# Second feed-forward of a routed macaron block: dispatched rows carry the residual, finished rows are scattered into the output, and one accumulating DMA closes it

## The reference, cut to what matters

```
def ffn(x, up, gate, down, router, w_up_s, w_gate_s, w_down_s):   # 8 experts, hidden 256
    idx = argmax(x @ router.T)                 # one expert for each row
    y  = (silu(x @ gate[idx].T) * (x @ up[idx].T)) @ down[idx].T
    ys = (silu(x @ w_gate_s.T) * (x @ w_up_s.T)) @ w_down_s.T      # shared expert, all rows
    return y + ys

x = x + 0.5 * ffn(layernorm(x), ...)
x = x + attn(layernorm(x), ...)                # attn(z) = z + gate * circular mixing of a decayed sum over t
x = x + 0.5 * ffn(layernorm(x), ...)
```

## Time and profile before

| | |
|---|---|
| the three times | 354.20, 349.97, 352.72 us; median 352.72 |
| span of the profiled execution | 305.8 us |
| median less that span | 46.9 us |
| mean granted clock of TensorE | 0.952 |
| PE, DVE, ACT, POOL busy in the span | 254.6, 187.3, 161.7, 194.1 us |
| DMA | 28.34 MB |

### The profile page before, as it was taken

The page is one execution under the profiler, slowest core; times in us unless marked ns, Lnnn a source line. Parts: engine busy times, 40 slices in busy tenths (PEclk is TensorE's granted clock), DMA queues, the critical chain, the costliest instruction groups (busy, mean ns, idle before and its releaser), DMA issues.

```text
span 305.8 us, 7883 instructions
## 1 busy us (share of the span) xinstructions
PE 254.6 (83%) x1788; PEld 213.2 (70%) x1788; DVE 187.3 (61%) x723; ACT 161.7 (53%) x376; POOL 194.1 (63%) x307
## 2 busy tenths in 40 slices
PE   0588999945999999994589888989779999999950
PEld 0446777535999999963468666757479989999540
DVE  4267574951565656537799999776646655565334
ACT  2455544232676777622769777940357766675100
POOL 3358887760478788861365888877408868788500
PEclk9999999995999999998957999999999999999976
DMA  7861111322223332218100111112322323332198
GB/s 201 287 287 35 46 43 46 102 71 62 58 86 97 88 97 87 78 46 248 28 3 1 35 38 35 47 45 70 101 64 80 90 72 96 87 96 64 48 289 253
DMA packets 34990, 28.34 MB, mean 93 GB/s; under 512 B 4784, under 2 KB 31792, under 8 KB 34704
## 3 DMA queue, kind: packets, MB, share of 16 engines
q1 hardware_dynamic: 25328, 16.06, 18.7%
q0 software_dynamic: 4544, 9.45, 8.6%
q10 hardware_dynamic: 5088, 2.50, 2.8%
HBM read 15.37 MB, written 12.62 MB: 92 GB/s over the span
## 4 chain that ended last, share of the span: by engine, by line
PE 42%; POOL 24%; DVE 10%; issue 9%; DMA 7%; ACT 3%; SPq 2%; DVEq 1%; POOLq 0%; ACTq 0%
PE bank L949 22%; POOL dispatched L374 15%; PE bank L959 9%; POOL scale_f L363 4%; PE bank L883 3%; PE bank L938 3%; POOL returned L404 2%; DMA back<-returned 2%; DVE xres L599 2%; DMA decay<-in_decay 2%; PE bank L895 1%; DMA returned<-ey,token 1%; PE bank L875 1%; DMA xs<-dispatched 1%; DVE hs L631 1%
## 5 line engine op out<-in xcount | busy, mean ns | idle before, releaser
L404 POOL DMA_INDIRECT returned<-ey,token x78 | 78.1, 1002 | 33.6 <-DVE ey L799 21.8
L949 PE MATMUL bank<-xsT,wgu 128*128 128x128 f32 x624 | 84.4, 280 | 2.8 <-ACT xsT L524 1.7
L949 PEld LDWEIGHTS bank<-xsT,wgu 128*128 128x128 f32 x624 | 77.0, 195 | 4.3 <-ACT xsT L524 1.5
L374 POOL DMA_INDIRECT dispatched<-xn,slot x64 | 63.9, 998 | 18.0 <-issue 18.0
L875 PE MATMUL bank<-xnT,gu 128*128 128x512 f32 x128 | 63.2, 620 | 4.6 <-DVE hs L631 3.7
L793 DVE TENSOR_TENSOR eh<-eg,bank 128x256 f32<-128x256 f32 x78 | 32.8, 421 | 49.3 <-ACT eg L531 36.5
L531 ACT ACTIVATE eg<-bank 128x256 f32<-128x256 f32 x78 | 29.9, 383 | 37.9 <-PE bank L949 37.7
L505 ACT ACTIVATE wgu<-gu 128x512 f32 x78 | 48.3, 624 | 0.9 <-issue 0.8
L959 PE MATMUL bank<-wdn,eh 128*128 128x128 f32 x312 | 47.4, 276 | 0.7 <-DVE ey L799 0.7
L480 ACT ACTIVATE sg<-bank 128x512 f32<-128x512 f32 x32 | 18.7, 589 | 49.2 <-PE bank L875 41.7
L883 PEld LDWEIGHTS bank<-dn,hs 128*128 128x128 f32 x256 | 33.4, 209 | 12.2 <-DVE hs L631 10.8
(11 more groups left out here) (100 smaller groups left out, 287.1 us busy)
## 6 DMA issues: line engine op xcount, KB each, us to landing
xs<-dispatched SPq DMA_DIRECT2D x80, 66.0 KB, 1.8
back<-returned SPq DMA_DIRECT2D x16, 256.0 KB, 5.4
gu<-in_gu SPq DMA_DIRECT2D x1, 2048.0 KB, 12.1
out<-xres ACTq DMA_DIRECT2D x8, 256.0 KB, 3.5
returned<-ey,token POOLq DMA_INDIRECT x78, 2.3
dn<-in_dn SPq DMA_DIRECT2D x1, 1024.0 KB, 10.9
dispatched<-xn,slot POOLq DMA_INDIRECT x64, 2.3
dispatched<-pads SPq DMA_DIRECT2D x10, 66.0 KB
```

The costliest lines, as they stand in the source:

```text
L374: nc.gpsimd.indirect_dma_start(dispatched[:, :], bass.IndirectOffsetOnAxis(slot[:, i:i + 1], 0), xn[:, i, :], None, bounds_check=last_row) ...
L404: nc.gpsimd.indirect_dma_start(returned[:, :], bass.IndirectOffsetOnAxis(token[:, s:s + 1], 0), ey[:, s, :], None, bounds_check=last_back) ...
L949: last = nc.tensor.matmul(bank[4 + s % WR][:, i * P:(i + 1) * P], wgu[:, s % WR, i * P:(i + 1) * P], xsT[:, s // 2 % 2, s % 2, :], start=T ...
```

## The change

- `xn` and `xres` become two parts of one buffer `rows`, 260 wide. There are two DRAM tensors, `dispatched[0]` with rows of 132 and `dispatched[1]` with rows of 260 that carry normed row, number and residual.
- In the second feed-forward the residual that is sent must hold the shared expert's result. So `parts_at(1, ...)` gives each step three parts, 19 in the steps, and the last 5 stand before the experts; none stands behind. POOL sends group k in step k+2 for k below 6, waiting for `half_done`; group 6 in step 7 ahead of group 5; group 7 last. Groups 6 and 7 are sent with a residual that has no shared part yet: their shared results go to `shared_late`.
- In both feed-forwards there are no tokens: the scatter of block b takes its index straight from `xs`. Pad rows all have the number N and are dropped by the bounds check. A block beyond the real ones loads 128 dummy rows. `load_block` waits `blk_out[s]` (the scatter of the slot's earlier block has landed) where it waited `blk_tok`.
- In the second, DVE evicts 0.5 y + residual, and the scatter goes to the output itself. Loads of `back`, adds and stores go. POOL waits for all scatters, and adds `shared_late` to groups 6 and 7 of the output with one accumulating DMA.

```diff
+WIDE = ROW + C
+DUMMY = E * CAP
+LATER_STEP = 3
+BASED = G - 2
+BEFORE = 3 * BASED + 1
...
+        rows = sb("rows", [P, NT, WIDE])
+        xn, xres = rows[:, :, 0:ROW], rows[:, :, ROW:WIDE]
+        shared_late = sb("shared_late", [P, (G - BASED) * TPG, C])
...
-        def parts_at(k, i):
-
-            return SHARED_PARTS[PER_STEP * (k - 1) + i:][:1] if 1 <= k < G else []
+        def parts_at(f, k, i):
+
+            if not 1 <= k < G:
+                return []
+            if f == 0:
+                return SHARED_PARTS[PER_STEP * (k - 1) + i:][:1]
+            first = LATER_STEP * (k - 1)
+            cut = (first, first + 1, first + LATER_STEP)
+            return SHARED_PARTS[cut[i]:min(cut[i + 1], BEFORE)]
+
+        def parts_before(f):
+
+            return (SHARED_PARTS[EARLY:LATE] if f == 0 else SHARED_PARTS[BEFORE:])
...
@@ load_block (SP)
                 wait_pos(sp, blk_turn, f * (NBL // 2) + (j - 1) * PAIRS + s // 2 + 1)
                 stand(sp)
-                first_use = is_int(j) and j == 0
-                wait_pos(sp, blk_tok, f * NB if first_use else f * NB + b - BU + 1)
+                wait_pos(sp, blk_out[s], (f * slot_blocks(s) + j) * 16)
                 stand(sp)
                 if row is None:
                     row = block_row(b)
-                sp.dma_start(xs[:, s, :], dispatched[bass.ds(row, P), :]).then_inc(blk_in[s], 16)
+                sp.dma_start(xs[:, s, 0:row_width(f)], dispatched[f][bass.ds(row, P), :]).then_inc(blk_in[s], 16)
...
                 sp.wait_ge(pads_at, f + 1)
-                send_pads(sp, range(0, PADS_SP))
+                sp.dma_start(dispatched[f][DUMMY:DUMMY + P, :], pads[:, 0:row_width(f)]).then_inc(pad_sent, 16)
+                send_pads(sp, f, range(0, PADS_SP))
...
-                for k in range(G):
-                    sp.dma_start(tiles(back, k),
-                                 returned_tiles[:, k * TPG:(k + 1) * TPG, :]).then_inc(back_in[k], 16)
-            sp.wait_ge(stored, 16 * G)
+                if f == 0:
+                    for k in range(G):
+                        sp.dma_start(tiles(back, k),
+                                     returned_tiles[:, k * TPG:(k + 1) * TPG, :]).then_inc(back_in[k], 16)
+            sp.wait_ge(stored, 16)
...
@@ POOL: scatter, middle, experts
                 pool.wait_ge(slotted, f * G + k + 1)
+                if f == 1 and k < BASED:
+                    pool.wait_ge(half_done, G + k + 1)
...
-                if valid(k):
-                    scatter(1, k)
+                if k == G - 1:
+                    scatter(1, BASED)
+                if 0 <= k - 2 < BASED:
+                    scatter(1, k - 2)
...
-                def tokens(j, s):
-
-                    pool.wait_ge(blk_in[s], (f * LOADS + j + 1) * 16)
-                    wait_pos(pool, blk_out[s], (f * slot_blocks(s) + j) * 16)
-                    nc.gpsimd.tensor_tensor(token[:, s:s + 1], xs[:, s, C:C + 1].bitcast(I32),
-                                            to_replica[:, bass.ds(j * BU + s, 1)], ALU.add).then_inc(blk_tok, 1)
-
-                def send(j, s):
-                    pool.wait_ge(blk_tok, f * NB + j * BU + s + 1)
+                target = out_rows if f else returned[:, :]
+
+                def send(j, s, more=True):
                     pool.wait_ge(blk_y, f * NB + j * BU + s + 1)
                     stand(pool)
                     nc.gpsimd.indirect_dma_start(
-                        returned[:, :], bass.IndirectOffsetOnAxis(token[:, s:s + 1], 0),
-                        ey[:, s, :], None, bounds_check=last_back).then_inc(blk_out[s], 16)
+                        target, bass.IndirectOffsetOnAxis(xs[:, s, C:C + 1].bitcast(I32), 0),
+                        ey[:, s, :], None, bounds_check=last_token, oob_is_err=False).then_inc(blk_out[s], 16)
...
             steps(middle, 4)
+            for k in range(BASED + 1, G):
+                scatter(1, k)
             experts(1)
+            for s in range(BU):
+                pool.wait_ge(blk_out[s], 16 * slot_blocks(s) * 2)
+            pool.wait_ge(half_done, 2 * G)
+            nc.gpsimd.dma_start(out_dram[:, BASED * TPG:NT, :], shared_late[:], accum_op=ALU.add).then_inc(stored, 16)
...
@@ ACT, end
-            for g, part in SHARED_PARTS[LATE:]:
-                shared(1, g, part)
-            for k in range(G):
-                act.wait_ge(x3_done, k + 1)
-                act.dma_start(out_dram[:, k * TPG:(k + 1) * TPG, :], tiles(xres, k)).then_inc(stored, 16)
...
@@ DVE: add_shared, tables, evac_y
-                add_half(k, by_tile(o_ps[:]), half_done)
+                if n >= G and k >= BASED:
+                    nc.vector.tensor_scalar(tiles(shared_late, k - BASED), by_tile(o_ps[:]), 0.5, None,
+                                            ALU.mult).then_inc(half_done, 1)
+                else:
+                    add_half(k, by_tile(o_ps[:]), half_done)
...
-                link(nc.vector.tensor_scalar(last_blk[:], blk_end[:, E - 1:E], -1.0, None, ALU.add))
-
-                link(nc.vector.tensor_scalar(real_blk[:], block_no[:], last_blk[:], None, ALU.min))
...
-                    nc.vector.tensor_copy(ey[:, s, :], bank[2 + s % 2][:, 0:C]).then_inc(blk_y, 1)
+                    y = bank[2 + s % 2][:, 0:C]
+                    if f == 0:
+                        nc.vector.tensor_copy(ey[:, s, :], y).then_inc(blk_y, 1)
+                    else:
+
+                        nc.vector.scalar_tensor_tensor(out=ey[:, s, :], in0=y, scalar=0.5, in1=xs[:, s, ROW:WIDE],
+                                                       op0=ALU.mult, op1=ALU.add).then_inc(blk_y, 1)
...
@@ DVE, end
-            for g, part in SHARED_PARTS[LATE:-2]:
-                shared(1, g, part)
-            for k in range(G):
-                add_back(1, k, x3_done)
-                if k < 2:
-                    shared(1, *SHARED_PARTS[k - 2])
...
@@ PE, experts
-                pe.wait_ge(half_done, f * G + parts_done(LATE, down=True))
-                pe.wait_ge(mult_done, f * G * HH + parts_done(LATE, down=False))
+                done = len(SHARED_PARTS) if f else LATE
+                pe.wait_ge(half_done, f * G + parts_done(done, down=True))
+                pe.wait_ge(mult_done, f * G * HH + parts_done(done, down=False))
```

More of the change, by code:

```diff
@@ L685, in front @@
                     stats_of(kind, later, later)
[L686 removed]
+                for g, part in parts_at(f, k, 0):
                     shared(f, g, part)
@@ L694, in front @@
                     pads_behind(f)
-                for g, part in parts_at(k, 1):
+                for g, part in parts_at(f, k, 1):
                     shared(f, g, part)
@@ L888, in front @@
                 n, q = f * G + k, k % 2
-                for g, part in parts_at(k, 0):
+                for g, part in parts_at(f, k, 0):
                     shared(f, g, part)
```

85 lines of the change are left out of this document (35 added, 50 removed).

## The result

The kernel after takes **392.76 us** (median of 4, 390.59 to 399.92), the kernel before 352.06 us in the same set (4, 349.97 to 354.20): ratio 1.1166, 95% interval 1.1103 to 1.123. It is slower by 40.7 us; the forecast was 390, in a range of 372 to 403. Ratios here are those of the faster executions of both kernels and medians are of all executions, so the two can differ by about a percent.

The account below looks back on a forecast made before the run. PE was taken to bound both expert phases at about 2.9 us a turn (two blocks). From 352.7 us, -0.8 + 17.9 - 1.5 + 15.9 + 17.9 - 12.2 = +37.2 gave 390 us, range 372 to 403.

Parts of the forecast that it names:

- the 1.5 us of the last scatters: End of each expert phase: without tokens POOL's last three scatters start earlier, saving 1.5 us.
- 46.9 us lie around the span: Whole kernel before: median 352.7 against a profiled span of 305.8; the 46.9 us outside it taken as unchanged.
- The ring: Both expert phases: loads wait for the scatter eight blocks earlier to land, so PE waits; +17.9 us each.
- The stretch of 8.0 us: Expert phases: two turns, each of two blocks, take 8.0 us through the chain of waits, where they took 5.8.
- rival C: Expert phases: PE's clock falls because PE waits; 416 us throughout, 399 for a third of the time; 12%.
- The 0.2 us for the wider load: Second expert phase: loads of 133 KB instead of 66 KB add 0.2 us, making the two-turn time 8.2.
- The second routing stage: Before the second expert phase: three shared parts a step and later scatters cost +15.9 us, bounds +9 to +19.
- POOL is now what the stage ends on: End of second routing stage: POOL's last dispatch scatter decides, the first gate/up following about 6 us behind it.
- The tail: From the last eviction to the end: 9.9 us in place of 22.1, -12.2, with 6 for the accumulating DMA.
- A: Expert phases: loads come in time, so waiting for landed scatters costs nothing; 353 us, or 346; 5%.
- B: Expert phases: the wait for landed scatters binds only half, two turns taking 6.9 us; 371 to 373 us; 15%.
- D: Tail: the accumulating DMA or the scatters in `out` are slow, 13 us and more; 397 us; 8%.

Follow-up runs that it names:

- narrow rows: Kernel after with all rows of the second exchange 528 bytes wide, the eviction adding the normalised input instead of the residual: 388.78 us, ratio 1.0803.
- the moved parts: Kernel before with three shared parts a step in the second feed-forward and none behind the experts, scatters in their old steps: 359.5 us, ratio 1.0253.
- the ring alone: Kernel before with one edit: a load waits for the landed scatter of the slot's earlier block instead of its token: 373.56 us, ratio 1.058.
- the ring undone: Kernel after with POOL copying the index to a token again, so loads no longer wait for landed scatters: 366.67 us, ratio 1.0495.
- before run again: Kernel before, unchanged, profiled once more: 350.78 us, ratio 1.0002, span 346.8.

## Why the prediction was right, and where it was not

**The sum.** Slower, by about the measured amount, and for the reason that was named first: that is right. The closeness of 390 to 392.8 owes something to luck. With the borders of the table its terms are -0.8, +16.4, +15.9, +16.4 and -10.7 (the 1.5 us of the last scatters counted to the second expert phase). Measured are 0, +14.7, +21.1, +13.1 and -6.8: the expert phases were forecast 5.0 us too dear, the rest 9.9 too cheap, and half of the errors cancel.

**The baseline.** "46.9 us lie around the span" was wrong; 41 of them are inside ordinary executions, in part as the stops and slow queue instructions shown above. The median came out close all the same, because the kernel after has time of this kind too. But the expert phases of 63 us from which the forecast counted are 79 in ordinary executions. That part of what the ring adds disappears in waits that are there anyway would explain why they grew less than forecast; no run shows it.

**The ring** was the right mechanism: the loads wait for landings, PE waits 35.7 us at the turn (34 forecast), the one line alone gives +20 us and its undoing -24 to -26. The stretch of 8.0 us was mis-sized: it is 9.73, against terms taken from the earlier trace rows. Term by term:
- transpose to the end of the eviction: 3.95, not 2.77. Both PE groups in this term run at the lower clock behind the wait (0.50 in the row above). To the start of the down group it is 2.03 instead of 1.33, with a gate/up of 1.97 where a turn without a wait has 1.06; from there to the eviction's end 1.90 instead of 1.44, with a down group of 1.06 instead of 0.61. This is the mechanism of rival C inside the ring, 1.2 of the 1.75 us by which the stretch was too short.
- eviction to scatter: 0.74, not 0.04. I had read it from a scatter in front of which POOL had been idle for 0.16 us. The trace of before has the right row elsewhere; here POOL had stood for 8 us, and 78.50+0.28 to 79.55 is 0.77:

```profile
78.50 0.28 DVE L799 COPY ey<-bank 128x128 f32<-128x128 f32 x1
...
79.55 0.99 POOL L404 DMA_INDIRECT returned<-ey,token  x1 [8.28 <-DVE ey L799]
```

- landing 2.24 (2.24), SP 0.99 (0.98), load 1.81 (1.95): right.

From 98 to 122 us PE waits at every other turn for 2.2 to 2.9 us; over both phases it is 25 waits of 1.4 on average, not 32 of 1.1. The sums are nearly the same. Against the ordinary before the phases grew by 14.7 and 13.1, where 17.9 less 1.5 was forecast for each: a longer ring on a longer base. The 0.2 us for the wider load did not show: the two phases are equally long (93.6 and 93.1), and narrow rows did not shorten the second.

**The second routing stage**: measured +21.1, forecast +15.9. The step of 8.95 was forecast as 8.7 and 8.5: right, and PE bound. "POOL is now what the stage ends on" failed, and the sign that the prediction had set for this, a shared part or DVE as the last thing PE waits for, is what the profile shows. In the kernel after the last scatter goes out at 271.87, SP's first load only at 280.00, and the first gate/up follows the last shared part, not a load:

```profile
283.79 0.69 DVE L643 TENSOR_SCALAR shared_late<-bank 128x512 f32<-128x512 f32 x1 [0.75 <-PE bank L891]
...
284.60 1.58 PE L957 MATMUL bank<-xsT,wgu 128*128 128x128 f32 x12 [0.63 <-DVE shared_late L643]
```

That is 12.7 us behind the last scatter, not 6.1; in the other profiles of this dispatch 7.5 to 13.1. The path that the term left out is PE's logits and the stops in DVE's last step, then ACT's pads, then the silus and the last five shared parts, which need 11.4 us from ACT's first silu. By run the moved parts explain 12.6 of the 21.1, 10 of them in the six steps; the rest is located in front of that silu and its cause is open.

**The tail**: -6.8 by the stage, -6.9 from the last eviction, forecast -12.2. Before, it was 20.3 us from the last eviction's end in an ordinary execution, not 22.1; after it is 13.4, not 9.9. The last scatter starts 2.2 us behind the last eviction, not 1.5. The accumulating transfer was sized rightly as 6 us. What the term mostly left out is ahead of it, in the chain of the kernel after:

```profile
377.70 2.08 DMA out<-ey,xs
...
380.02 0.55 issue
380.57 1.69 POOLq L96
```

0.8 us from the landing to POOL's instruction, and 1.7 for the instruction, before the 6.3 us begin. The rule of the Trainium skill, "DMA: Bandwidth & Descriptors", section on the anatomy of one DMA on the gpsimd path, which the prediction set beside it, gave 3.2 us for these 512 KB, an estimate by that page. The trace does not agree for the accumulating transfer, which is on the gpsimd path and takes 6.3 us. The plain write, which takes 3.3, is from SP's queue and thus no measurement of that path.

**The rivals.** A (the ring does not bind) fell by the ring alone. B (a stretch of 6.9 us, 371 to 373) is out with a stretch of 9.73. C holds in part: the clock in the phases is 0.87 and 0.91 against 0.98 and 0.94, and 1.00 and 0.95 when the ring is undone, and a waited-for turn costs about 1.2 us more through it, the difference worked out above. The prediction's sentence that the trace of before has both levels at similar busy shares misreads: the mean clock of 0.79 stands beside 5.28 us of 8, the 1.00 beside 6.88 of 8 and 6.58 of 7. D (a transfer of 13 us) is out, with 6.8 at most in any profile.

Nothing tried beats the kernel before. With the ring undone, what is left over it is the third part of a step and the 8 us at the end of the stage, against 6.4 saved in the tail.

## What to carry to other kernels

Before a buffer's release is moved from a copy to a landed DMA, add up the ring, link by link, from rows in which each engine was really waiting, and include what stands ahead in its queue: a link read from a busy engine hides the wake of 0.7 us. Take the time of PE's groups in the ring from rows behind a wait as well: here they took nearly twice as long there. Work that leaves the tail must fit somewhere; three parts in a step made PE the bound of the stage's steps and cost 10 us there, against 6.8 saved in the tail. And look at the time beside the span of the same execution before anything is added to a median.

## What the runs showed of the hardware that was not expected

- From the end of an eviction to the scatter of a POOL that had stood for over 1 us it is 0.75 to 0.80 us in 50 of 51 cases: 2 in the short execution of before, 12 in before run again, 37 in the kernel after.
- A wait of PE of 2.5 us, with a granted clock of 0.97 up to its end, was followed by 3.0 us at 0.50: eight matmuls took 1.97 us instead of 1.06.
- Ordinary executions hold stops of 4 to 11 us on ACT and DVE at once, near the same steps of most kernels (the moved parts lack that of the second stage), and queue instructions of 0.7 us that usually take 0.03. One execution of the kernel before had no such stop of DVE and no such instruction in SP's loads, and its span was 41 us shorter. Their cause is open.
- Accumulating 512 KB in DRAM from POOL's queue took 6.2 to 6.8 us to land (eight profiles), a plain write of the same from SP's 3.3.
- Two transfers of 2 MB from DRAM to DRAM in rows of 512 bytes held a pad in the same queue for 21.9 and 24.5 us.
